# A zero-point product hoisted out of a 16-step loop, with bf16 transposes and earlier loads of x, in an attention and quantized-FFN layer on eight cores

## What is computed

```python
xn = _layernorm(x, axis=-1)
x = x + attn(xn, Wq, Wk, Wv, Wo) + ffn(xn, wq_gate, s_gate, wq_up, s_up, wq_down, s_down)
```

```python
def _qlinear(x, wq, scale):
    W = (wq.astype(jnp.float32) - ZERO_POINT) * scale[:, None]   # ZERO_POINT = 128
    return jnp.einsum('bsd,hd->bsh', x, W)
ffn = _qlinear(silu(_qlinear(xn, wq_gate, s_gate)) * _qlinear(xn, wq_up, s_up), wq_down, s_down)
```

## Time and profile before

| | us |
|---|---|
| runs of the kernel | 3143.45 and 3149.18, median 3146.31 |
| the profiled execution, time | 3145.17 |
| its span on the slowest core (core 6) | 3143.3 |
| spans of the eight cores | 3132.0 to 3143.3 |
| TensorE busy on core 6 | 2981.8, 95% of the span |
| mean granted TensorE clock | 0.968 |

### The profile page before, as it was taken

The page is one execution under the profiler, slowest core; times in us unless marked ns, Lnnn a source line. Parts: engine busy times, 40 slices in busy tenths (PEclk is TensorE's granted clock), DMA queues, the critical chain, the costliest instruction groups (busy, mean ns, idle before and its releaser), DMA issues.

```text
span 3143.3 us, 34289 instructions; the slowest of 8 cores (3132.0 to 3143.3 us)
## 1 busy us (share of the span) xinstructions
PE 2981.8 (95%) x14127; PEld 1393.8 (44%) x14387; DVE 412.0 (13%) x959; ACT 526.0 (17%) x809; POOL 160.1 (5%) x306
## 2 busy tenths in 40 slices
PE   4999999999999999999949999999999999999998
PEld 2444454444444444444424444544444444444443
DVE  4101170000000001010131101700000000001010
ACT  4000072221122100000040000721222111000000
POOL 0000000000000001000000000000000000000000
PEclk9999979999999999999969999699999999999999
DMA  5222201222222244463462222012222122434543
GB/s 136 81 81 69 79 15 57 78 81 76 72 81 80 74 154 149 143 227 142 159 161 68 80 81 71 11 67 75 73 81 80 68 81 72 175 139 168 213 147 145
DMA packets 50071, 321.14 MB, mean 102 GB/s; under 512 B 5808, under 2 KB 5863, under 8 KB 22272
## 3 DMA queue, kind: packets, MB, share of 16 engines
q0 software_dynamic: 42816, 268.60, 24.1%
q1 hardware_dynamic: 4672, 33.56, 3.5%
q10 hardware_dynamic: 2432, 16.78, 1.9%
HBM read 209.86 MB, written 16.78 MB: 72 GB/s over the span
## 4 chain that ended last, share of the span: by engine, by line
PE 91%; ACT 3%; DMA 2%; issue 2%; DVE 2%; ACTq 0%; DVEq 0%; POOL 0%; POOLq 0%; SPq 0%
PE p L594 39%; PE p L421 21%; PE p L694 19%; PE p L679 7%; PE p L388 1%; PE pb L646 1%; ACT xn_b L326 1%; PE pb L463 1%; DMA dwst<-wd 1%; PE p L702 1%; DVE rs L548 1%; PE p L514 0%; PE pb L521 0%; DMA xbuf<-x 0%; DMA wst<-wo 0%
## 5 line engine op out<-in xcount | busy, mean ns | idle before, releaser
L594 PE MATMUL p<-xnT,wst 128*128 128x512 bf16 x5518 | 1214.5, 380 | 6.3 <-issue 0.4
L594 PEld LDWEIGHTS p<-xnT,wst 128*128 128x128 bf16 x5632 | 552.5, 98 | 668.1 <-issue 7.1
L421 PE MATMUL p<-xnT,wst 128*128 128x512 bf16 x3010 | 661.0, 379 | 3.6 <-issue 0.4
L694 PE MATMUL p<-actT,dwst 128*128 128x512 bf16 x2760 | 619.0, 381 | 13.1 <-DMA dwst<-wd 9.3
L421 PEld LDWEIGHTS p<-xnT,wst 128*128 128x128 bf16 x3072 | 301.0, 98 | 363.2 <-issue 2.1
L694 PEld LDWEIGHTS p<-actT,dwst 128*128 128x128 bf16 x2816 | 276.2, 98 | 346.7 <-issue 18.2
L679 PE MATMUL p<-attnT,wst 128*128 128x512 bf16 x996 | 230.9, 382 | 8.6 <-DVE lo_b L396 4.0
L614 DVE TENSOR_TENSOR actT<-gate_b,up_b 128x512 bf16<-128x512 bf16 x176 | 74.9, 425 | 1152.3 <-ACT up_b L609 1152.3
L603 ACT ACTIVATE gate_b<-p,sgT 128x512 bf16<-128x512 f32 x176 | 120.9, 687 | 491.0 <-PE p L594 491.0
L609 ACT ACTIVATE up_b<-p,suT 128x512 bf16<-128x512 f32 x176 | 121.0, 687 | 474.5 <-PE p L594 474.5
L706 ACT ACTIVATE outT<-p 128x512 f32<-128x512 f32 x64 | 38.2, 597 | 898.1 <-PE p L679 898.1
(11 more groups left out here) (72 smaller groups left out, 881.1 us busy)
## 6 DMA issues: line engine op xcount, KB each, us to landing
wst<-wgu POOLq DMA_DIRECT2D x88, 1024.0 KB, 5.1
dwst<-wd POOLq DMA_DIRECT2D x128, 704.0 KB, 4.1
wst<-wo POOLq DMA_DIRECT2D x32, 1024.0 KB, 6.0
wst<-wq POOLq DMA_DIRECT2D x16, 1024.0 KB, 5.1
wst<-wk POOLq DMA_DIRECT2D x16, 1024.0 KB, 5.0
wst<-wv POOLq DMA_DIRECT2D x16, 1024.0 KB, 5.0
out_nat<-x SPq DMA_DIRECT2D x4, 4096.0 KB, 19.8
y<-out_nat SPq DMA_DIRECT2D x8, 1024.0 KB, 9.4
```

The costliest lines, as they stand in the source:

```text
L421: e.matmul(o, s, r, start=stt, stop=sp),
L594: e.matmul(o, s, r, start=stt, stop=sp),
L694: e.matmul(o, s, r, start=stt, stop=False),
```

## The change

- The zero-point product (L702) no longer stands in the loop over `oc`. Once for each `tb`, ahead of both loops, the same product of hilo_xn with the -128 tile goes alone into a bank of its own (pb6, pb7), and ScalarE copies it to SBUF as corr_sb[tb] in f32. These two products wait for hilo2, the copied low rows.
- In each block, L706 on ScalarE becomes a VectorE instruction: outT = corr_sb * s_down + wobank. The second one (L712) stays, and both now write bf16.
- outT is bf16, and its transposes use eye_b and write bf16 into pb4 or pb5.
- `emit_x` has other waits in the second chunk: for the slots xbuf0 and xbuf1 it waits until the dwst and outT buffers are read, for xstg0 and xstg1 until actT and the attention's buffers are. No load of x waits for the stores of y any more. The writes into xnT still do.
- The two small masks come as bf16 from the host, and the two casts on VectorE (L231, L232) are gone.

```diff
-            w = mx(xslot_free[xs], st_["out_store"] if c > 0 else None,
-                   (st_["attn_pe_done"] if (c > 0 and xs >= 2) else None),
-                   (st_["actT_read"] if (c > 0 and xs >= 2) else None))
+            if xs < 2:
+                w = mx(xslot_free[xs],
+                       (dslot_free[0] if c > 0 else None),
+                       (dslot_free[1] if c > 0 else None),
+                       (st_["outT_free"][0] if c > 0 else None),
+                       (st_["outT_free"][1] if c > 0 else None))
+            else:
+                w = mx(xslot_free[xs],
+                       (st_["attn_pe_done"] if c > 0 else None),
+                       (st_["actT_read"] if c > 0 else None))
...
+        for tb in range(2):
+            pcb = [pb6, pb7][tb]
+            pcf = [pf6, pf7][tb]
+            t_cm = P.add("tensor",
+                         lambda e, o=pcf[0:128, 0:512], s=cneg[:], r=hilo_ac[:, tb * 512:(tb + 1) * 512]:
+                         e.matmul(o, s, r, start=True, stop=True),
+                         waits=mx(hilo2, tok_cneg, bank_free[id(pcb)]), inc="ST")
+            t_ce = P.add("scalar",
+                         lambda e, o=corr_sb[tb][:], s=pcf[0:128, 0:512]: e.activation(o, s, AF.Copy),
+                         waits=mx(t_cm, st_["corr_free"][tb]), inc="SS")
...
-                                 e.transpose(o, s, eye_f[:]),
+                                 e.transpose(o, s, eye_b[:]),
...
-                t_dn = P.add("tensor",
-                             lambda e, o=dbank[:], s=cneg[:], r=hilo_ac[:, tb * 512:(tb + 1) * 512]:
-                             e.matmul(o, s, r, start=False, stop=True),
-                             waits=mx(hilo2, tok_cneg), inc="ST")
-                last_dn = t_dn
+                last_dn = t_dmm
                 ot = outT0 if oc % 2 == 0 else outT1
-                t_cp = P.add("scalar", lambda e, o=ot[:], s=wobank[:]: e.activation(o, s, AF.Copy),
-                             waits=mx(t_mm, st_["outT_free"][oc % 2], st_["ln_xbuf_done"],
-                                      st_["attn_scr_free"]), inc="SS")
+                t_cp = P.add("vector",
+                             lambda e, o=ot[:], s0=corr_sb[tb][:], sc=sdT[:, oc:oc + 1],
+                                    s1=wobank[:]:
+                             e.scalar_tensor_tensor(o, s0, sc, s1, ALU.mult, ALU.add),
+                             waits=mx(t_mm, corr_toks[tb], tok_sd,
+                                      st_["outT_free"][oc % 2], st_["ln_xbuf_done"],
+                                      st_["attn_scr_free"]), inc="SV")
```

More of the change, by code:

```diff
@@ L151, in build_program @@
     eye_b = ata("eye_b", [128, 128], BF16, 256)
-    mkA_f = ata("mkA_f", [9, 128], F32, 512)
-    mkB_f = ata("mkB_f", [9, 512], F32, 2048)
     mkA = ata("mkA", [9, 128], BF16, 256)
@@ L185, in build_program @@
     pf5 = pb5[:].bitcast(F32)
+    pf6 = pb6[:].bitcast(F32)
+    pf7 = pb7[:].bitcast(F32)
     PBF = [p0, p1, p2, p3]
@@ L217, in build_program @@
         "outT_free": [None, None],
+        "corr_free": [None, None],
     }
@@ L225, in build_program @@
     tok_scl = ("dsl", P.cnt["dsl"])
-    P.add("gpsimd", lambda e: e.dma_start(mkA_f[:], dmska), inc="dmk", amt=16)
-    P.add("gpsimd", lambda e: e.dma_start(mkB_f[:], dmskb), inc="dmk", amt=16)
-    tok_mask = ("dmk", P.cnt["dmk"])
+    P.add("gpsimd", lambda e: e.dma_start(mkA[:], dmska), inc="dmk", amt=16)
+    P.add("gpsimd", lambda e: e.dma_start(mkB[:], dmskb), inc="dmk", amt=16)
+    tok_mk = ("dmk", P.cnt["dmk"])
     tok_eyeb = P.add("vector", lambda e: e.tensor_copy(eye_b[:], eye_f[:]),
                      waits=mx(tok_eye), inc="SV")
-    P.add("vector", lambda e: e.tensor_copy(mkA[:], mkA_f[:]), waits=mx(tok_mask), inc="SV")
-    tok_mk = P.add("vector", lambda e: e.tensor_copy(mkB[:], mkB_f[:]), waits=mx(tok_mask), inc="SV")
     tok_eps = P.add("vector", lambda e: e.memset(eps_t[:], EPS), inc="SV")
@@ L628, in out_phase @@
         last_dn = None
+        corr_toks = [None, None]
+        for tb in range(2):
[8 more added lines that the diff above has]
+                         waits=mx(t_cm, st_["corr_free"][tb]), inc="SS")
+            bank_free[id(pcb)] = t_ce
+            corr_toks[tb] = t_ce
         for tb in range(2):
@@ L685, in out_phase @@
                 wt22 = mx(d_tok1)
+                t_dmm = None
                 for hc in range(HCN):
@@ L692, in out_phase @@
                                          r=actT[:, hc * 1024 + tb * 512: hc * 1024 + tb * 512 + 512],
-                                         stt=(hc == 0):
-                                  e.matmul(o, s, r, start=stt, stop=False),
+                                         stt=(hc == 0), sp=(hc == HCN - 1):
+                                  e.matmul(o, s, r, start=stt, stop=sp),
                                   waits=(wt if hc == 0 else (wt22 if hc == 22 else [])), inc=inc)
@@ L712, in out_phase @@
                              e.scalar_tensor_tensor(o, s0, sc, s1, ALU.mult, ALU.add),
-                             waits=mx(t_dn, t_cp, tok_sd), inc="SV")
+                             waits=mx(t_dmm, t_cp, tok_sd), inc="SV")
                 bank_free[id(dbank)] = t_st
@@ L716, in out_phase @@
                     do_tail2(*pend[0])
-                pend[0] = (ot, pf4 if oc % 2 == 0 else pf5,
+                pend[0] = (ot, pb4 if oc % 2 == 0 else pb5,
                            pb4 if oc % 2 == 0 else pb5, t_st, oc)
             do_tail2(*pend[0])
+            st_["corr_free"][tb] = t_cp
             wst_toks = mx(*add_toks)
@@ L793 @@
     C = float(2 ** 43)
-    mska = np.ones((9, 128), dtype=np.float32)
-    mskb = np.full((9, 512), -C, dtype=np.float32)
+    mska = np.ones((9, 128), dtype=ml_dtypes.bfloat16)
+    mskb = np.full((9, 512), -C, dtype=ml_dtypes.bfloat16)
     for r in range(8):
-        mska[1 + r] = (idx % 8 == r).astype(np.float32)
-        mskb[1 + r] = np.tile((idx % 8 == r).astype(np.float32) * C, 4)
+        mska[1 + r] = (idx % 8 == r).astype(ml_dtypes.bfloat16)
+        mskb[1 + r] = np.tile(((idx % 8 == r) * C).astype(ml_dtypes.bfloat16), 4)
     mskb[0] = -C
```

11 lines of the change are left out of this document (6 added, 5 removed).

## The result

The changed kernel takes 3112.88 us (median of 9 runs) against 3144.87 before (median of 8). The ratio is 0.9896, with a 95% interval from 0.9884 to 0.9909: 1.04% faster, 32 to 33 us, where 1.3% and 3103.4 us were forecast. In some executions the cores of one die run at a lower clock; these are left out of the ratios and of the times in the experiments (without them the two medians above are 3112.4, of 6 runs, and 3144.3, of 6), and where only one or two runs are left, the text gives them.

The account below looks back on a forecast made before the run. TensorE bounds the kernel, with 91% of the chain. Sum: -26.2 - 16.0 + 1.4 + 1.0 + 1.5 - 3.5 = -41.8 us, from 3145.2 to 3103.4 us, 1.3% faster; range 3092 to 3119.

Parts of the forecast that it names:

- A: Rival: DMA takes the gain back, +9 for the new products, +5 for growing waits, 0 for x; 3118 us, chance 0.12.
- B: Rival: bf16 transposes bring nothing, only the zero-point products' removal gains; 3119 us, chance 0.10.
- The zero-point products and the transposes: Output blocks: 64 zero-point products at 0.41 us go, -26.2; 64 sets of transposes in bf16 save 0.25 each, -16.0.
- the +1.4 for the ends of the halves: Four ends of a half: the last transposes wait for L712, so 0.34 us of saving is taken back at each.
- The wait for the low row: Ahead of the blocks: hoisted products wait for the low row's DMA, +1.0 us, bounds -1 and +9.
- the cover: Existing weight waits hide the new wait: first chunk 3.89 us plus 2.4 of half clock, second only 0.93 us.
- The sign of being wrong that I had set for the cover: Output phases: waits for weights adding up to over 15 us, against 13.5 before, would show the cover wrong.
- Waits that grow back: Start of each chunk's second half: TensorE arrives earlier and waits longer for weights, +1.5 us, between 0 and +5.
- The loads of x: Between the chunks: loads issued earlier, served behind the stores, save a round trip, -3.5 us; bounds -11.9 and 0.
- the bound that I had named for 0: Loads of x between the chunks: no gain if the stores were slowed as much as the loads gain.
- C: Rival: between the chunks x comes beside the stores, -11.9 instead of -3.5; 3095 us, chance 0.12.
- D: Rival: TensorE's clock falls at the new wait and stays at 1.2 GHz; 3168 us with five blocks, chance 0.02.

Follow-up runs that it names:

- the run with needless products: Changed kernel with 15 unused one-column products on TensorE between the column sum and the hoisted products, while the low row's DMA is under way; 3106.08 us in one run.
- The version with the late products: Changed kernel with the two hoisted products put behind the first block's 16 Wo products instead of ahead of them; 3102.62 us, ratio to before 0.9869.
- stores in groups: Changed kernel with hoisted products behind the first Wo products, and each half's stores of y issued in four groups of four output blocks; 3081.05 us, ratio to before 0.9801.

## Why the prediction was right, and where it was off

The time lies in the range, and the sign came out. Of the forecast 41.8 us, 32 to 33 came. The blocks came as forecast, and three other terms all erred to the same side; the range held because its upper end was drawn for the rivals A and B. Step by step:

*The zero-point products and the transposes, -26.2 and -16.0: right.* A block takes 13.17 us, forecast 13.19. The two alone took 0.46 and 0.26 off a block, forecast 0.41 and 0.25, and the transposes in place stand at 0.23. Alone they add up to a little more than together (0.72 against 0.68): behind the zero-point product the bf16 set saves 0.26, behind the down products only 0.44 - 0.22. By an estimate from the 81 ns or so that the Trainium skill's page TensorE: Matmul & The Clock Gate, section Back-to-back issue gap, gives for each matmul of 128 columns in a stream, the four would have needed some 0.32; the trace disagrees with that figure, and the measurement decides. 64 blocks at 0.68 are -43.5, with the +1.4 for the ends of the halves -42. A first half without a wait says the same: 223.4 us before, 212.9 with the change (the run with needless products), 10.5 less, four times -42.

*The wait for the low row, +1.0: the step that failed.* Its parts were right: 3.52 us idle (forecast 3.5), the first Wo product 2.7 us later instead of 2.1, the clock falling to 1.2 GHz, at 2.2 us a chunk instead of 2.4 (the run with needless products parts the two). What was wrong is the cover. I took it from core 6 alone: 3.89 us of waiting for a down piece, and 2.4 of half clock behind that. Core 6 was the slowest, and its wait there was the longest. Two of the other cores, before the change:

```profile
1130.55 9.66 PE L694 MATMUL p<-actT,dwst 128*128 128x512 bf16 x44 [2.43 <-DMA dwst<-wd]
...
1130.32 11.34 PE L694 MATMUL p<-actT,dwst 128*128 128x512 bf16 x44 [3.16 <-DMA dwst<-wd]
```

Core 1 waits 2.43 us and keeps the full clock, core 4 waits 3.16 and loses it for a part of the 44. In all, three cores waited 2.4 to 2.6 us at this place without half clock behind it, two 3.2 and 3.4 with it, and two less than 1 us. So the first half of the first chunk took 226.1 us in the median, and such a half takes 223.4 where it has no wait (the shortest four in the second chunk: 223.2 to 223.4), so only 2.7 us of cover were there instead of 6.3 (3.9 and 2.4), and in the second chunk 0.3 instead of 0.9. That makes 2.7 + 2.1 - 2.7 in the first and 2.7 + 2.2 - 0.3 in the second, +6.7 instead of +1.0. The version with the late products, 6.5 us faster in these stages, bears out the size. The sign of being wrong that I had set for the cover, over 15 us of waits for weights in the output phases, did not show it: the changed kernel's slowest core has 11.4. That sum tells which waits are left, not how much cover there had been.

*Waits that grow back, +1.5: right in kind, too small.* Without any wait a second half would take 211.8 us (measured without the load of x). The changed kernel needs 219.5 and 219.5, so 15.4 us of waits and half clock in the two. For the kernel before the same count is 16 x 13.85 with 0.49 less in its first block and 1.1 more at its tail, 222.3, which leaves 4.2 and 8.3, 12.5. So +2.9. That most of them come from the 4 MB load of x is shown by the run without it.

*The loads of x, -3.5: wrong, +0.4 in the changed kernel, -0.6 alone.* The order of service was as I had it, behind the stores, and the loads now follow the stores without the pause of before. What I had at no change is the stores: they land at 12.2 us after their issue before, at 16.4 now. This is the bound that I had named for 0, "if the stores were slowed as much as the loads gain". Two windows show it, of the kernel before and of the changed one (columns as in the earlier trace rows), both inside the time in which the stores are under way:

```profile
1573.00:1577.00 4.00, 0.00 (x0) 0.00 (x0) 0.00 (x0) 0.00 (x0) 0.00 (x0) 0.50 1.01 401
...
1556.00:1560.00 4.00, 0.00 (x0) 0.00 (x0) 0.00 (x0) 0.00 (x0) 0.00 (x0) 0.50 1.04 178
```

The DMA engines are full in both, but they move 178 GB/s in the second, at a share of 1.04, and 401 in the first, at 1.01. The last stores of the changed kernel land at about 1564.2 (1548.0 + 16.2), behind this window, and the loads stand behind them in both queues, so it is the stores that are slow in it. In both kernels the first tile is there some 20 us after the stores' issue. Why stores slow down when loads are queued behind them, on this core and on the seven others, was not tried. The Trainium skill's page DMA: Bandwidth & Descriptors, section Queues, rings and completion order, says that each DMA engine consumes a queue's descriptors in ring order. The runs agree: with x ahead of the stores the first statistics start 6.9 us after their issue, with x behind them 20.

*The end: +1.1, not forecast.* The last stores take 13.0 us instead of 12.0. The eight cores now end within 8.4 us instead of 11.3, so more of them may store at once; this is not shown.

*The rivals.* A, that DMA takes it back, is what happened in part: its terms +9, +5 and 0 add up to 14 where 10.0 were measured (6.7, 2.9 and 0.4), and the forecast's to -1.0; only for the waits that grow back (2.9) was the forecast's 1.5 nearer. B falls by the run with the transposes alone, C by the loads alone, and D did not occur: the half clock lasted 5 us in each chunk.

The sum as measured: -42 + 6.7 + 2.9 + 0.4 + 1.1 = -30.9, which is the table's.

## What to carry to other kernels

A small product that is hoisted out of a loop takes its wait along: place it where the engine has other work in front of it, not at the head of the queue. Look for the cover of a new wait on all cores and not on the slowest alone, whose stalls are part of what made it the slowest. A transfer issued earlier behind a full queue landed no earlier here; what helps is to have less in front of it, and that was worth more here (22 us for stores in groups) than the new waits of the loads of x, which gave nothing.

## What the hardware showed that I had not expected

A matmul with two rows between matmuls of 128 rows costs 0.41 us in its block, 0.46 with f32 transposes behind it, twice what its 512 columns need; the two steps, in and out, are half of it. An idle stretch of 3.5 us on TensorE costs 2.2 us more than its length, as the 5 us of work behind it go at 1.2 GHz, and 15 needless products in it win that back; of two cores that waited 3.09 and 3.20 us at one place, only the first lost its clock. And 4 MB of stores take 15 to 16 us to land instead of 12 when loads of x are queued right behind them, with the DMA engines full and at one stretch at 178 GB/s.
